# The side chain's pieces in an LSTM's steps: one place on VectorE instead of two

## The reference, cut to what matters

```python
def step(carry, xw_t):
    prev_h, prev_c = carry
    a = xw_t + prev_h @ Wh
    i = jax.nn.sigmoid(a[:, :Hdim])
    f = jax.nn.sigmoid(a[:, Hdim:2 * Hdim])
    o = jax.nn.sigmoid(a[:, 2 * Hdim:3 * Hdim])
    g = jnp.tanh(a[:, 3 * Hdim:])
    next_c = f * prev_c + i * g
    next_h = o * jnp.tanh(next_c)
    return ((next_h, next_c), next_h)
...
x = x + _L0_attn_ref(_L0_cond_ref(x, cond_1024[:, None, :], ...), ...)
x = x + _L0_ffn_ref(_L0_cond2_ref(x, cond_1024, ...), ...)
```

## Time and profile before

| | us |
|---|---|
| median of 3 runs | 605.9 (604.86 to 606.87) |
| the profiled execution | 606.4 |
| its span, from the first to the last instruction | 604.6 |

### The profile page before, as it was taken

How to read it: one execution, slowest core, us unless ns; L and a number is a source line. 1 busy time by engine, 2 the same in 40 slices (tenths; PEclk the granted TensorE clock), 3 DMA queues, 4 the chain that set the end, 5 groups by cost and what they waited for, 6 DMA issues and landing times.

```text
span 604.6 us, 16158 instructions
## 1 busy us (share of the span) xinstructions
PE 419.0 (69%) x6261; PEld 324.2 (54%) x6261; DVE 379.9 (63%) x2221; ACT 238.2 (39%) x928; POOL 20.5 (3%) x31
## 2 busy tenths in 40 slices
PE   3453866687655987995367676776867674897996
PEld 2233644475544755874345454554655463676774
DVE  8888248258777656467755766667666766444442
ACT  1247866425334344234233333343343333332332
POOL 8021000000000000000000000000000000000000
PEclk9577886587555555555555555555555555556555
DMA  7300000000000000000000000000000000000000
GB/s 192 84 0 1 3 3 1 1 1 2 1 2 2 3 1 2 1 3 1 2 2 2 2 3 2 2 2 2 2 2 3 1 3 2 7 5 6 10 6 9
DMA packets 8824, 5.71 MB, mean 9 GB/s; under 512 B 1988, under 2 KB 8236, under 8 KB 8748
## 3 DMA queue, kind: packets, MB, share of 16 engines
q1 hardware_dynamic: 7564, 3.77, 2.5%
q10 hardware_dynamic: 1184, 0.92, 0.5%
HBM read 4.15 MB, written 0.52 MB: 8 GB/s over the span
## 4 chain that ended last, share of the span: by engine, by line
PE 38%; DVE 36%; ACT 19%; issue 7%; DMA 1%; ACTq 0%; DVEq 0%
PE bank L1704 15%; ACT h_fac L790 7%; DVE h_off L1342 5%; DVE pr L1335 5%; ACT gates L788 5%; PE bank L1531 5%; DVE gates L1338 4%; DVE h_fac L1336 3%; DVE mx L1275 2%; PE bank L1604 2%; PE bank L1499 2%; PE bank L1442 2%; PE bank L1506 1%; ACT ta L777 1%; PE bank L1569 1%
## 5 line engine op out<-in xcount | busy, mean ns | idle before, releaser
L1704 PE MATMUL bank<-h_off,wha 128*128 128x4 f16 x1020 | 68.8, 172 | 117.1 <-DVE h_off L1342 112.3
L1704 PEld LDWEIGHTS bank<-h_off,wha 128*128 128x128 f16 x1020 | 51.7, 109 | 172.3 <-DVE h_off L1342 168.4
L788 ACT ACTIVATE gates<-bank 128x16 f32<-128x16 f32 x256 | 47.1, 184 | 167.4 <-PE bank L1704 166.6
L1335 DVE SCALAR_TENSOR_TENSOR pr<-gates 128x8 f32<-128x8 f32 x256 | 42.4, 166 | 89.9 <-ACT gates L788 88.4
L790 ACT ACTIVATE h_fac<-gates 128x4 f32<-128x4 f32 x256 | 53.1, 207 | 113.5 <-DVE gates L1338 113.5
L1342 DVE TENSOR_TENSOR h_off<-h_fac 128x4 f16<-128x4 f32 x256 | 43.2, 169 | 63.9 <-ACT h_fac L790 63.5
L1704 PE MATMUL bank<-h_low,wha 128*128 128x4 f16 x1020 | 63.6, 167 | 0.0
L1704 PE MATMUL bank<-h_off,whb 128*128 128x4 f16 x1020 | 62.7, 166 | 0.0
L1344 DVE TENSOR_TENSOR_SCAN h_low<-h_fac,h_off 128x12 f16<-128x12 f32 x256 | 46.6, 182 | 8.7
L1531 PE MATMUL bank<-kT,qz 32*128 32x32 f32 (+7 forms) x256 | 51.1, 530 | 0.8 <-ACT kT L754 0.8
L1704 PEld LDWEIGHTS bank<-h_low,wha 128*128 128x128 f16 x1020 | 47.0, 105 | 0.0
(11 more groups left out here) (285 smaller groups left out, 731.0 us busy)
## 6 DMA issues: line engine op xcount, KB each, us to landing
x_tm<-in_x ACTq DMA_DIRECT2D x1, 512.0 KB, 5.2
x_tb<-in_x SPq DMA_DIRECT2D x4, 128.0 KB, 2.7
wf<-in_L_cond_w_f SPq DMA_DIRECT2D x2, 256.0 KB, 3.3
out_y<-tb SPq DMA_DIRECT2D x7, 64.0 KB, 2.0
ada_w<-in_L_cond_w_ada SPq DMA_DIRECT2D x1, 384.0 KB
ada_b<-in_L_cond_b_ada ACTq DMA_DIRECT2D x1, 384.0 KB, 5.8
w1s<-in_L_ffn_w SPq DMA_DIRECT2D x1, 256.0 KB
w2s<-in_L_ffn_w SPq DMA_DIRECT2D x1, 256.0 KB
```

The lines of the kernel that those rows point to most:

```text
L788: nc.scalar.activation(gates[:, k, 0:GW], src, ACT.Tanh, scale=1.0 / A_SCALE).then_inc(gates_act, 1)
L1335: V.scalar_tensor_tensor(pr[:, k, :], gates[:, k, B:3 * B], 1.0, gates[:, k, 3 * B:5 * B], ALU.add, ALU.mult).then_inc(p_ready, 1)
L1704: ins = T.matmul(acc[:, g * B:(g + 1) * B], w[:, g, :], h, start=False, stop=True, skip_group_check=True)
```

## The change

```diff
@@ -1336,7 +1336,6 @@
                 V.tensor_scalar(h_fac[:, k, :, 2], gates[:, k, 0:B], 1.0, 0.5 * H_SCALE, ALU.add, ALU.mult)
                 vec.wait_ge(p_ready, t + 1)
                 V.scalar_tensor_tensor(gates[:, 1 - k, 4 * B:5 * B], pr[:, k, B:2 * B], 0.5, pr[:, k, 0:B], ALU.mult, ALU.add).then_inc(c_new, 1)
-                rest.go(t, 1)
 
                 vec.wait_ge(th_act, t + 1)
                 V.tensor_tensor(h_off[:, k, :, 2], h_fac[:, k, :, 2], h_fac[:, k, :, 1], ALU.mult).then_inc(h_ready, 1)
@@ -1348,7 +1347,7 @@
                 for c, i in attending(t):
                     attend(c, i)
                     jobs += 1
-                rest.go(t, 3 if jobs == 0 else 2)
+                rest.go(t, 4 if jobs == 0 else 3)
                 for p, i in feeding(t):
                     if i == 5:
                         result(p)
```

## The result

The median of the changed kernel is 609.4 us (607.3 to 610.6, 7 runs) against 606.1 (604.9 to 606.9, 7 runs): a ratio of 1.0057, with a 95% interval of 1.0038 to 1.0075. That is 3.3 us more. The profiled execution took 607.3 us, the shortest of the seven, and that needs care: its span of 605.5 us is only 0.9 above the span before. Both kernels in stretches, first the one before: the steps with side chain (0 to 79), steps 80 to 221, steps 222 and 223, and the rest.

The account below looks back on a forecast made before the run. No engine is full; the recurrence's step-to-step loop of 1.60 us bounds the kernel. Terms -1.45 + 2.52 + 2.12 = +3.2 us take the median from 605.9 to 609.1 us, range 606.8 to 610.8.

Parts of the forecast that it names:

- The spacing of instructions: VectorE queue: an instruction occupies its duration less 0.08 us; a dependent one starts 0.03 to 0.04 us after the other's end.
- the room of 0.60 us: VectorE's free time from the history product's issue (L1346) to the next L1335; any overrun delays the next step one for one.
- The squares: L1218, waiting for ScalarE, no longer delays the high part: steps 42 (0.96 us) and 39 (0.49) gain, 37 and 46 nothing.
- Wide pieces: Pieces of 128 columns and more overrun in steps 2 to 4, 18, 21, 22, 28, 60, 65, 78: +2.52 us together.
- Small pieces: Small pieces overrun in steps 0, 8 to 11, 13, 17, 19, 20, 27, 54, 66, 73, 76, 77: +2.12 us.
- The cover in steps 16 and 26: TensorE works on attention past the late high part there, so VectorE's lateness is free; nothing lost in 15 and 25.
- Small overruns: Rival, 13 in 100: the recurrence absorbs overruns of 0.05 to 0.2 us, giving 607.0 us.
- Faster: Rival, 5 in 100: overruns are covered, freed high parts alone are worth 3.05 us, giving 602.9 us.
- the time doesn't change: Rival, 2 in 100: the order of instructions changes but the time stays 605.9 us.
- queue of another engine: Rival, 8 in 100: ScalarE or TensorE waits in its queue for later results, gates slip up to 1.6 us: 610.7 us.
- The 3.2 us: Summed slowdown, predicted as growth of the distance from the gate activation of step 0 to that of step 79.
- Nothing changes behind it: From step 79 on VectorE has no pieces left, so 295 us of the span were to stay unchanged.

Follow-up runs that it names:

- the two squares: Kernel before, with only the squares of steps 39 and 42 (L1218) moved behind the low part: median 602.8 us, ratio 0.9952.
- the three parts: Kernel before, moving behind the low part only the squares of steps 39 and 42 (602.8 us), only small pieces (607.8) or only wide pieces (607.9).
- the run of 609.2 us: The changed kernel run once more, unaltered, for another profile: 609.2 us.

## Why the prediction was right

It gave 609.1 us with 606.8 to 610.8, and the median is 609.4. The mechanism holds term by term, as the steps below show. That the median came within 0.3 us is luck in part: the medians of single experiments lie up to 1.9 us off what the same sums gave (604.7 expected for the two squares, 602.8 measured). By its steps:

- **The spacing of instructions and the room of 0.60 us.** Right, and now measured by itself: three chained small instructions fit, the fourth costs 0.05.
- **The squares, -1.45 us.** Measured alone: -1.42. The forecast that in step 39 TensorE's own work takes over from the wait was right: the recurrent matmul comes 1.43 us after the gate activation, as put. In steps 37 and 46 nothing was gained, as said.
- **Wide pieces, +2.52 us.** Measured alone: +2.50.
- **Small pieces, +2.12 us.** Measured alone: +2.24. Every step behind one of the list is longer, by 0.05 to 0.27 us, and none other. This term was 0.12 too small: steps 10, 14, 18, 28, 77 and 78 are each 0.01 to 0.02 longer than put, and the rest is scattered.
- **The cover in steps 16 and 26.** Steps 15, 16, 25 and 26 are as long as before. That rests on the profiles; no run was made for it.
- **The rivals.** Small overruns are not absorbed (+2.24 alone). *Faster* and *the time doesn't change* needed the overruns to be covered, and they were not. No queue of another engine was held up: the three parts add up to the whole, and no step outside the list moved.
- **One place was put wrongly.** The 3.2 us were promised between the gate activations of steps 0 and 79. There they are 2.86; 0.44 more fall into step 79, whose L1335 is late through the overrun of step 78, so the sum holds at step 80: 3.30.
- **"Nothing changes behind it" was wrong for single executions.** The higher clock of steps 222 and 223 is worth 2.1 us, two thirds of the whole effect, and it was there in the profiled run after and not in the one before. Only one of the seven runs has a profile; it is the shortest by 2.0 us, so the median probably stands for the lower clock, as the run of 609.2 us does.

## What to carry to other kernels

In a loop of short steps in which one engine serves a recurrence and side work, draw up the free gaps of a quiet step and the length of what is to go in: 0.36 and 0.60 us here. The side work that waits for nothing belongs in every gap up to its size, the one that may wait for another engine behind the recurrence's last instruction, and moving all of it to one gap throws the other away. A table by step beat both rules here: it spread the wide pieces over neighbouring steps whose gaps are empty, and put two small ones in the middle gap where a job fills the rear one.

Compare such a change over the stretch that it touches. Spans of two single executions hid two thirds of the effect.

## What the runs showed of the hardware

- A VectorE instruction of 128x4 numbers that waits for the one before starts 0.19 us after it, one that doesn't 0.07 to 0.08: 0.74 us for four chained, 0.52 for six free.
- In nine profiles the same TensorE-bound steps 222 and 223 took 5.44 to 5.45 us five times, with a granted clock of 0.50 (1.2 GHz), 3.33 us three times, at 1.00 (2.4 GHz), and 3.82 once, at 0.85. The same program showed both (609.2 and 607.3 us). By the records TensorE was busy throughout steps 220 and 221 in all of them (2.41 and 2.21 us long, against 1.60 of a quiet step). The clock rose at the end of step 221 in three, inside step 222 in one, at the end of step 223 in one, and not at all after the start of the recurrence in the other four. What decides this is not settled here; that the two fastest kernels had it in their profiles may be chance.
- The part ahead of the recurrence took 160.56 us in one of nine profiles and 157.0 to 157.4 in the others, with the same instructions: 32 matmuls took 3.73 us in the profile before and 5.58 in this one, where the granted clock fell to 0.51 from 126 us on and was 1.00 in the other. Why it fell is open.
